# Sorting edges in a graph network: row one-hots turned from key columns by TensorE, lane one-hots scaled by ScalarE, and one block for ranks, placement and scatters

## The chip, the core and the metric

The kernel runs on one core of a Trainium2 chip. The metric is the device time of one execution in microseconds (us). A core has five engines with instruction streams of their own: TensorE (PE; its weight loads are listed as PEld), VectorE (DVE), ScalarE (ACT), GpSimd (POOL) and SyncE (SP). They meet only through semaphores. A DMA is issued from an engine's queue and runs beside the engines.

## The reference, cut to what matters

```
x:   (6250, 128) float32          src: (100000,) int32, random in 0..6249
dst: (100000,) int32 in 0..6249, sorted, dense at small numbers
edge_index = jnp.stack([src, dst])
h = jnp.maximum(_layernorm(x, axis=-1), 0.0)
x = x + _L0_gnn_ref(h, edge_index, ...)   # two GATv2 layers with self loops, softmax and sum over dst
h = jnp.maximum(_layernorm(x, axis=-1), 0.0)
x = x + _L1_gnn_ref(h, edge_index, ...)   # 8-head attention, sum over src (rows = edge_index[0])
```

The first part sums over the edges of each destination, the second over the edges of each source. The kernel therefore first brings the edges into two orders. Nothing of this order is in the reference: it is the kernel's way of doing the segment sums, and the change touches this sort alone.

## The kernel before, in words

The 100,000 edges lie as 800 columns of 125 edges, with the edge inside a column on the partition. A node number is split in a block (the number divided by 128, 49 of them) and a lane (the remainder). `sort_by_dst` finds for every edge a slot in a table in DRAM, `rec_by_dst`, in which the edges of a block of destinations lie together. It works in blocks of the program (`with nc.Block()`); every engine waits at the end of each for all others.

1. Keys are loaded and turned (about 8 to 28 us of the span), then counted (to 205 us), then tables are made (to 213 us).
2. **The ranks**, L448 to L578. A *half* is four columns, and there are 200 halves. For each half, VectorE makes one-hots in two layouts: `key_columns` (L538) compares a row of keys that SyncE has broadcast to all partitions with the partition's number (lane on the partition, edge along the row, 128x512), and `one_hots` (L529, through the helper's L301) compares keys on the partition with a row of numbers (edge on the partition), for the lanes (125x512) and for the blocks (125x196). TensorE matches the key columns with themselves (`match_keys`), adds the half to a running table (`update`), looks slots up in the table (`look_up`) and adds what lies earlier in the same column (`count_earlier`). ScalarE rounds the table (`round_table`, L476) and turns the match into 0 and 1 (`mark_earlier`, L466). VectorE takes the table's remainder (`split_table`, L551), multiplies the looked-up rows with the block one-hot (`read_table`, L558) and sums them to slots (`slots`, L564). `ranked` is raised by one with each half.
3. **Scans**, `SortBySrc.on_vector` and its sisters, in the same block after the ranks: for each of the 49 blocks of sources ScalarE makes a one-hot of 125x800, VectorE scans (L696) and multiplies (L699) it, and TensorE adds it up.
4. **The placement**, `SortBySrc.permute`, in a block of its own: for each of the 800 columns VectorE makes two lane one-hots, each multiplied with one piece of the edge's record (L763, 125x128), and a tile one-hot (L765, 125x832), and TensorE multiplies them in four matmuls (L805). This is the order by source, kept in SBUF.
5. **The scatters**, on POOL's queue. 49 indirect DMAs (L574) write the self loops' records into `rec_by_dst`. Then `Records.write` (L593) issues 800 indirect DMAs (L600), one for each column, 125 records of 8 bytes each. A scatter waits for its half's `ranked`, and for the scatter 16 before it to have landed. 320 of them are issued in the block of ranks and scans, the other 480 in the block of the placement.

What sets the order on each engine is the code's order. `pipeline` runs a list of stages for each half or column with a lead: a stage with lead 1 works on the next half. The first and last turns are unrolled, the rest is a loop of 8 halves (4 columns in the placement). No planner moves anything.

Each engine stalls only at its own waits, so the end of a block is the latest end of POOL's scatters, VectorE's chain, and what hangs on it. After the sort come the two graph layers, which read `rec_by_dst`.

## Time and profile before

| | us |
|---|---|
| median of 3 runs (7204.37, 7215.49, 7318.86) | 7215.49 |
| the profiled execution's own time | 7202.38 |
| its span, from the first to the last instruction | 7200.5 |
| the sort's last two blocks (ranks and scans; placement) | 213 to 926 and 926 to 1686 |

A row of a timeline gives start, duration, engine, line, operation, out<-in with shapes, the count of instructions merged in the row, and in brackets the idle time before it with what ended it. "issue" is idle time for which the profile shows no releaser. "remote" is a releaser that the profile does not see on the core's own engines at that moment. An instruction's duration can overlap the next one's start on the same engine, so a step of a loop is read from start to start. A window row gives, for a stretch of the span, each engine's busy time and in brackets its number of instructions, then the granted TensorE clock as a share of 2.4 GHz, the DMA engines' busy share and GB/s.

### The profile page before, as it was taken

The page shows a single profiled execution, that of the slowest core. Times are in us where ns is not written, and L with a number is a line of the kernel's source. Part 1 is how long each engine was busy: PE and PEld are TensorE (multiplying, and loading weights), DVE is VectorE, ACT ScalarE, POOL GpSimd, SP SyncE. Part 2 cuts the span into 40 slices and gives each one's busy share as a digit, 9 for nine tenths or more (in the row PEclk, how much of TensorE's full clock was granted, in tenths as well). Part 3 has the DMA queues.
Part 4 walks back from the last instruction along what each step waited for, and adds up shares of the span by engine and source line. Part 5 has one row for each costly group of instructions (what it writes and reads, how often), then busy time and mean ns, then how long its engine had stood idle before and what let it go on. Part 6 is the DMA issues. An engine that isn't in the chain of part 4 may idle for free. (4 is left out here: it accounts for less than half of the span.)

```text
span 7200.5 us, 128816 instructions
## 1 busy us (share of the span) xinstructions
PE 5138.8 (71%) x22244; PEld 2877.3 (40%) x22245; DVE 5824.7 (81%) x13976; ACT 3716.2 (52%) x17417; POOL 3967.3 (55%) x3546
## 2 busy tenths in 40 slices
PE   3386589972588898988877889889885555445452
PEld 2254233321244444444443444444443344444442
DVE  9596899972599999999848999999996455555556
ACT  5142500001399999999738999999993200000000
POOL 0688868882266666656305665666650255555552
PEclk9975899985799999999989999999997776776765
DMA  0234000001355555555424555555560233333333
GB/s 12 31 66 47 6 1 1 1 3 41 113 138 139 138 140 140 140 138 139 77 71 130 139 139 139 139 138 140 139 126 21 79 95 97 96 97 97 98 96 59
DMA packets 397679, 657.24 MB, mean 91 GB/s; under 512 B 141671, under 2 KB 259365, under 8 KB 396947
## 3 DMA queue, kind: packets, MB, share of 16 engines
q0 software_dynamic: 185888, 481.62, 27.2%
q1 hardware_dynamic: 211442, 172.59, 9.9%
q14 instruction: 326, 2.66, 0.2%
q8 instruction: 23, 0.38, 0.0%
HBM read 617.73 MB, written 33.88 MB: 90 GB/s over the span
## 5 line engine op out<-in xcount | busy, mean ns | idle before, releaser
L1209 POOL DMA_INDIRECT feat_area<-xl_table,feat_area x1856 | 1984.9, 1069 | 1721.1 <-PE bank L1283 680.1
L1360 ACT ACTIVATE feat_area<-feat_area 128x130 f32<-128x130 f32 x5568 | 1642.7, 297 | 181.2 <-issue 119.3
L1270 PE MATMUL bank<-node_area,feat_area 128*128 x3712 | 1470.2, 519 | 353.8 <-DVE feat_area L1405 158.5
L1344 ACT ACTIVATE feat_area<-feat_area 128x128 f32<-128x128 f32 x4640 | 1443.0, 387 | 64.6 <-issue 64.4
L1283 PE MATMUL bank<-feat_area 128*128 128x390 f32 x3712 | 1408.5, 502 | 68.1 <-ACT feat_area L1344 21.8
L1772 POOL DMA_INDIRECT feat_area<-kv_table,feat_area x832 | 809.8, 973 | 899.7 <-DVE feat_area L1869 352.5
L600 POOL DMA_INDIRECT rec_by_dst<-feat_area,gather_col x800 | 1123.0, 1404 | 281.3 <-issue 240.1
L1360 ACT ACTIVATION_READ_ACCUMULATOR feat_area<-feat_area 128x1 f32 x5568 | 1040.0, 187 | 26.9 <-issue 26.4
L1270 PEld LDWEIGHTS bank<-node_area,feat_area 128*128 128x128 f32 x3712 | 637.4, 191 | 997.9 <-issue 732.5
L1405 DVE TENSOR_TENSOR feat_area<-bank,feat_area 128x780 f32<-128x780 f32 x928 | 886.0, 955 | 65.1 <-remote 41.0
L1283 PEld LDWEIGHTS bank<-feat_area 128*128 128x128 f32 x3712 | 666.6, 190 | 645.8 <-issue 246.3
L1810 PE MATMUL bank<-feat_area 128*128 128x136 f32 x1664 | 388.9, 403 | 714.0 <-DVE feat_area L1869 672.4
L1413 DVE SCALAR_TENSOR_TENSOR feat_area<-feat_area 128x780 f32<-128x780 f32 x928 | 886.4, 955 | 0.0
L1822 ACT ACTIVATE feat_area<-feat_area 128x32 f32<-128x32 f32 x208 | 47.7, 229 | 1370.1 <-DVE feat_area L1857 754.0
L1886 DVE TENSOR_TENSOR node_area<-node_area,bank 128x136 f32 x832 | 242.5, 291 | 506.2 <-issue 160.6
L805 PE MATMUL bank<-feat_area 125*128 125x416 f16 x3200 | 636.5, 343 | 8.3 <-DVE feat_area L765 8.3
L1810 PEld LDWEIGHTS bank<-feat_area 128*128 128x128 f32 x1664 | 332.0, 288 | 764.2 <-DVE feat_area L1869 355.8
L1452 DVE SCALAR_TENSOR_TENSOR node_area<-node_area,stays,bank 128x390 f32 x812 | 493.8, 608 | 21.1 <-PE bank L1283 20.3
L1010 ACT ACTIVATE node_area<-node_area 128x6272 f32<-128x6272 f32 x2 | 10.9, 5429 | 815.7 <-DVE node_area L976 815.7
L763 DVE TENSOR_SCALAR feat_area<-feat_area 125x128 f16<-125x128 f16 x1600 | 419.4, 346 | 0.3
L805 PEld LDWEIGHTS bank<-feat_area 125*128 125x128 f16 x3200 | 248.4, 98 | 396.6 <-DVE feat_area L765 185.7
L957 DVE TENSOR_TENSOR feat_area<-iota_f,lo_col 128x256 f32<-128x256 f32 x928 | 379.8, 409 | 0.0
(313 smaller groups left out, 6762.8 us busy)
## 6 DMA issues: line engine op xcount, KB each, us to landing
feat_area<-lo_slot SPq DMA_DIRECT2D x464, 128.0 KB
feat_area<-xl_table,feat_area POOLq DMA_INDIRECT x1856
feat_area<-lo_slot_src SPq DMA_DIRECT2D x208, 128.0 KB
node_area<-lo_edge SPq DMA_DIRECT2D x100, 256.0 KB
xl_table<-feat_area SPq DMA_DIRECT2D x98, 195.0 KB, 2.2
feat_area<-kv_table,feat_area POOLq DMA_INDIRECT x832
rec_by_dst<-feat_area,gather_col POOLq DMA_INDIRECT x800
feat_area<-gates SPq DMA_DIRECT2D x348, 32.0 KB
```

What stands on the lines that cost most here:

```text
L600: pool.indirect_dma_start(k.rec_d, bass.IndirectOffsetOnAxis(ap=self.pos[:, c:c + 1], axis=0), self.pay[:, c, :], None).then_inc(self.writ ...
L805: last = nc.tensor.matmul(out[n][m], self.to_lane[s][:, n * P:(n + 1) * P], self.to_tile[s][:, m * half:(m + 1) * half], start=False, stop ...
L1209: pool.indirect_dma_start(ring[:, at:at + HE], None, k.xl, bass.IndirectOffsetOnAxis(ap=index[s // CG][:, n:n + 1], axis=0)).then_inc(gath ...
L1270: last = nc.tensor.matmul(pair[s % 2][:, u, 0:HE], pick[s // 2 % 2][:, c:c + P], k.node[:, ds(columns[0], HE)], start=True, stop=True)
L1283: last = nc.tensor.matmul(sums_in[s % 2], place[s % 2][:, u * P:(u + 1) * P], ring[:, at:at + HE], start=u == 0, stop=u == GS - 1)
L1344: last = nc.scalar.activation(row[:, 0:D], row[:, 0:D], ACT.Copy, scale=row[:, D:D + 1])
L1360: last = nc.scalar.activation(at, at, ACT.Copy, accum_out=score[s // CG][:, to:to + 1])
L1405: nc.vector.tensor_tensor(z[s % V].rearrange("p (u e) -> p u e", u=GS), pair[s % 2][:, :, 0:HE], ring[:, s * W:(s + 1) * W].rearrange("p ( ...
L1413: nc.vector.scalar_tensor_tensor(out=zu, in0=zu, scalar=0.0, in1=att_w.unsqueeze(1).to_broadcast([P, GS, HE]), op0=ALU.max, op1=ALU.mult). ...
L1452: last = nc.vector.scalar_tensor_tensor(out=k.node[:, ds(to, HE)], in0=spare, scalar=k.stays[:, ds(g, 1)], in1=sums_in[s % 2], op0=ALU.mul ...
L1772: pool.indirect_dma_start(kv[s][:, u * KV:(u + 1) * KV], None, k.kv, bass.IndirectOffsetOnAxis(ap=index[s][:, u:u + 1], axis=0)).then_inc( ...
L1810: nc.tensor.matmul(k.bank[2 + u][:, 0:VW], place[s % 2][:, u * P:(u + 1) * P], wv[s % 2][:, u * VW:(u + 1) * VW], start=True, stop=True).t ...
```

## The change

Three edits are made together.

1. **Ranks.** VectorE no longer makes the 125x512 lane one-hot. TensorE turns it from the key columns (`flip_keys`, four matmuls with the identity into one of two banks) and ScalarE copies it from the bank to SBUF (`keep_rows`). The key columns are made two halves ahead, in four buffers in place of two.
2. **Placement.** VectorE makes one unscaled lane one-hot per column (`at_lane`); ScalarE multiplies it with each of the two pieces (`scale`), and TensorE waits for that as well.
3. **One block.** Placement runs behind ranks and scans in the same block on every engine, and POOL's 800 scatters follow each other without a block's end among them.

The diff, without regard to indentation, cut to its core:

```diff
-RANK_COLS = 320
...
-    oh_loT = [cut(HALF * P // 2, F16) for _ in range(2)]
+    oh_loT = [cut(HALF * P // 2, F16) for _ in range(4)]
...
+    flip = [k.bank[n][:, 0:HALF * P] for n in range(2)]
+    move_on_vector, move_on_scalar, move_on_tensor, move_on_sync = beside.permute()
...
+            def keep_rows(j, s):
+                h = R * j + s
+                act.wait_ge(flipped, h + 1)
+                if later(h, 2):
+                    act.wait_ge(updated, h - 1)
+                nc.scalar.copy(oh_lo[s % 2].rearrange("p u m -> p (u m)"), flip[s % 2]).then_inc(lo_set, 1)
...
-            pipeline(act, halves, [(0, round_table), (0, mark_earlier)], R)
+            pipeline(act, halves, [(0, round_table), (1, keep_rows), (1, mark_earlier)], R)
             beside.on_scalar(act)
+            move_on_scalar(act)
...
+            def flip_keys(j, s):
+                h = R * j + s
+                pe.wait_ge(ohT_ready, h + 1)
+                if later(h, 2):
+                    pe.wait_ge(lo_set, h - 1)
+                for u in range(HALF):
+                    last = nc.tensor.matmul(flip[s % 2][:, u * P:(u + 1) * P], oh_loT[s % 4][:, u * P:(u + 1) * P], eye,
+                                            start=True, stop=True)
+                last.then_inc(flipped, 1)
...
-            pipeline(pe, halves, [(0, update), (0, look_up), (0, count_earlier), (1, match_keys)], R)
+            pipeline(pe, halves, [(1, flip_keys), (1, match_keys), (0, update), (0, look_up), (0, count_earlier)], R)
             beside.on_tensor(pe)
+            move_on_tensor(pe)
...
-                c = snapped(dve, HALF * h)
-                one_hot_rows(oh_lo[s % 2], lo, c, P)
-                one_hot_rows(hi3[s % 2], hi, c, NB).then_inc(oh_set, 1)
+                one_hot_rows(hi3[s % 2], hi, snapped(dve, HALF * h), NB).then_inc(hi_set, 1)
...
-            pipeline(dve, halves, [(0, split_table), (-1, read_table), (1, key_columns), (-1, slots), (1, one_hots)], R)
+            pipeline(dve, halves, [(0, split_table), (-1, read_table), (2, key_columns), (-1, slots), (1, high_rows)], R)
             beside.on_vector(dve)
+            move_on_vector(dve)
...
-            records.write(pool, 0, RANK_COLS, ranked)
+            records.write(pool, ranked)
...
-                    for n in range(2):
-                        nc.vector.tensor_scalar(self.to_lane[s][:, n * P:(n + 1) * P], self.iota[:, 0:P],
-                                                self.lane_f[:, ds(c, 1)], self.piece[n][:, ds(c, 1)], ALU.is_equal, ALU.mult)
+                if later(c, 4):
+                    dve.wait_ge(scaled, c - 3)
+                nc.vector.tensor_scalar(self.at_lane[s], self.iota[:, 0:P], self.lane_f[:, ds(c, 1)], None, ALU.is_equal
+                                        ).then_inc(lane_set, 1)
...
+                pe.wait_ge(scaled, c + 1)
...
+            def scale(j, s, c):
+                act.wait_ge(lane_set, c + 1)
+                if later(c, 4):
+                    act.wait_ge(moved, c - 3)
+                for n in range(2):
+                    last = nc.scalar.activation(self.to_lane[s][:, n * P:(n + 1) * P], self.at_lane[s], ACT.Copy,
+                                                scale=self.piece[n][:, ds(c, 1)])
+                last.then_inc(scaled, 1)
...
-        by_src.permute(records)
```

How it moves instructions, first on VectorE, in one half of the ranks. Names that begin with `r_` are semaphores of that block (`r_looked` is raised by `count_earlier`, `r_bc0` by the landing of a broadcast key row). Line numbers of the changed kernel are its own. Before:

```order
L551 TENSOR_TENSOR node_area<-bank,node_area 128x196 [waits r_looked,r_coarse]
L558 TENSOR_TENSOR node_area<-bank,node_area 125x196 [waits r_ranked,r_looked]
L544 TENSOR_SCALAR node_area<-node_area,part_f 128x512 [waits r_bc0,r_looked]
L564 TENSOR_REDUCE gather_col<-node_area 125x4 [waits r_multiplied]
L301 TENSOR_TENSOR node_area<-iota_b,node_area 125x512 [waits r_multiplied,r_looked]
L301 TENSOR_TENSOR node_area<-iota_b,node_area 125x196
```

And now:

```order
L571 TENSOR_TENSOR node_area<-bank,node_area 128x196 [waits r_looked,r_coarse]
L578 TENSOR_TENSOR node_area<-bank,node_area 125x196 [waits r_ranked,r_looked]
L564 TENSOR_SCALAR node_area<-node_area,part_f 128x512 [waits r_bc0,r_looked]
L584 TENSOR_REDUCE gather_col<-node_area 125x4 [waits r_multiplied]
L300 TENSOR_TENSOR node_area<-iota_b,node_area 125x196 [waits r_multiplied,r_looked]
```

The 125x512 comparison is gone, the other five operations of a half stand in the same order, and the key columns (L564 of the changed kernel) are for one half later.

On TensorE, one half of the ranks before, from the match for the next half on (L490 and L493 match, L502 updates, L510 and L513 look up, L520 counts):

```order
L490 MATMUL bank<-node_area 128x512 [waits r_earlier,r_onehotT]
L493 MATMUL bank<-node_area 128x128 x4
L502 MATMUL bank<-node_area 128x49 [waits r_fine,r_onehot]
L502 MATMUL bank<-node_area 128x49 x3
L510 MATMUL bank<-node_area 128x196 [waits r_multiplied]
L513 MATMUL bank<-node_area 128x49 x8
L520 MATMUL bank<-node_area 128x49 [waits r_earlier]
L520 MATMUL bank<-node_area 128x49 x3
```

And now, from the flip on (L502 flips, L510 and L513 match, L523 updates, L531 and L534 look up, L541 counts):

```order
L502 MATMUL bank<-node_area 128x128 [waits r_lo_rows,r_onehotT]
L502 MATMUL bank<-node_area 128x128 x3
L510 MATMUL bank<-node_area 128x512 [waits r_earlier]
L513 MATMUL bank<-node_area 128x128 x4
L523 MATMUL bank<-node_area 128x49 [waits r_fine,r_lo_rows,r_onehot]
L523 MATMUL bank<-node_area 128x49 x3
L531 MATMUL bank<-node_area 128x196 [waits r_multiplied]
L534 MATMUL bank<-node_area 128x49 x8
L541 MATMUL bank<-node_area 128x49 [waits r_earlier]
L541 MATMUL bank<-node_area 128x49 x3
```

Four matmuls are added ahead of the match, with a wait for ScalarE's copy of two halves ago, and the update waits for `r_lo_rows`, ScalarE's copy for this half, besides VectorE's two results.

On VectorE in the loop of the placement, one column before (ISA rows load a column's number):

```order
L763 ISA [waits p_moved]
L763 TENSOR_SCALAR feat_area<-feat_area 125x128
L763 ISA
L763 TENSOR_SCALAR feat_area<-feat_area 125x128
L765 ISA
L765 TENSOR_SCALAR feat_area<-feat_area 125x832
L761 REGISTER_ALU
```

And now, with the beginning of the next column:

```order
L779 ISA [waits p_scaled,p_moved]
L779 TENSOR_SCALAR feat_area<-feat_area 125x128
L781 ISA
L781 TENSOR_SCALAR feat_area<-feat_area 125x832
L776 REGISTER_ALU
L779 ISA [waits p_scaled,p_moved]
```

One of three comparisons is gone, and there is a wait for ScalarE (`p_scaled`) beside the one for TensorE.

## Rows read from the trace of the kernel before

**Rows 1.** The page's head and part 1, busy time and share of the span.

```profile
span 7200.5 us, 128816 instructions
...
PE 5138.8 (71%) x22244; PEld 2877.3 (40%) x22245; DVE 5824.7 (81%) x13976; ACT 3716.2 (52%) x17417; POOL 3967.3 (55%) x3546
```

**Rows 2.** Windows: stretch, length, PE, PEld, DVE, ACT, POOL, clock, DMA, GB/s.

```profile
277.00:301.60 24.60, 2.05 (x22) 1.36 (x22) 2.08 (x7) 1.13 (x3) 14.16 (x12) 1.00 0.08 1
...
301.60:577.00 275.40, 230.89 (x3017) 153.47 (x3016) 274.98 (x825) 119.28 (x275) 233.32 (x139) 0.75 0.42 67
...
577.00:773.00 196.00, 116.16 (x1273) 77.91 (x1274) 119.84 (x345) 52.05 (x117) 157.93 (x126) 0.54 0.32 35
...
779.50:896.00 116.50, 65.56 (x156) 27.20 (x156) 113.74 (x80) 75.05 (x78) 104.51 (x40) 0.97 0.05 1
...
935.00:1572.00 637.00, 635.58 (x3197) 248.07 (x3198) 636.64 (x2401) 0.00 (x0) 514.78 (x402) 1.00 0.08 1
...
1584.00:1677.00 93.00, 0.00 (x0) 0.00 (x0) 0.00 (x0) 0.00 (x0) 73.87 (x63) 0.50 0.10 3
```

**Rows 3.** Timeline of POOL: three scatters, after two waits and the last.

```profile
301.63 1.18 POOL L600 DMA_INDIRECT rec_by_dst<-feat_area,gather_col  x1 [6.90 <-DVE gather_col L564]
...
927.38 1.30 POOL L600 DMA_INDIRECT rec_by_dst<-feat_area,gather_col  x1 [31.25 <-ACTq L737]
...
1680.03 1.18 POOL L600 DMA_INDIRECT rec_by_dst<-feat_area,gather_col  x1 [0.30 <-issue]
```

**Rows 4.** Timeline of DVE: its first instruction after the placement's block.

```profile
1686.35 0.17 DVE L1036 MEMSET feat_area<- 128x128 f32 x1 [102.56 <-PEq L737]
```

**Rows 5.** Timeline of DVE: one half of the ranks' even stretch.

```profile
481.08 0.95 DVE L301 TENSOR_TENSOR node_area<-iota_b,node_area 125x512 bf16<-125x512 bf16 x2
481.95 0.35 DVE L551 TENSOR_TENSOR node_area<-bank,node_area 128x196 f16<-128x196 f32 x1
482.23 0.34 DVE L558 TENSOR_TENSOR node_area<-bank,node_area 125x196 f32<-125x196 f32 x1
482.50 0.41 DVE L544 TENSOR_SCALAR node_area<-node_area,part_f 128x512 f16<-128x512 f16 x1
482.83 0.34 DVE L564 TENSOR_REDUCE gather_col<-node_area 125x196 f32 x1
```

**Rows 6.** Timeline of POOL: a scatter of the even, one of the uneven stretch.

```profile
481.11 1.70 POOL L600 DMA_INDIRECT rec_by_dst<-feat_area,gather_col  x1 [0.30 <-issue]
...
599.74 1.18 POOL L600 DMA_INDIRECT rec_by_dst<-feat_area,gather_col  x1 [0.30 <-issue]
```

**Rows 7.** Who waited for whom in the ranks' uneven stretch, 577 to 773.

```profile
ACT node_area L466 <- remote: 93.8, 31, 5.7
```

**Rows 8.** Timeline of PE: the four 128-wide matmuls of two matches.

```profile
501.63 0.39 PE L493 MATMUL bank<-node_area 128*128 128x128 f16 x4
...
597.12 0.63 PE L493 MATMUL bank<-node_area 128*128 128x128 f16 x4
```

**Rows 9.** Timeline of DVE: one block of the scans and the next's begin.

```profile
887.37 1.88 DVE L696 TENSOR_TENSOR_SCAN feat_area<-feat_area 125x800 f32<-125x800 f32 x1
889.29 0.99 DVE L699 TENSOR_TENSOR feat_area<-feat_area 125x800 f32<-125x800 f32 x1
890.31 1.88 DVE L696 TENSOR_TENSOR_SCAN feat_area<-feat_area 125x800 f32<-125x800 f32 x1
```

**Rows 10.** Timeline of DVE: one column of the placement.

```profile
1563.92 0.53 DVE L763 TENSOR_SCALAR feat_area<-feat_area 125x128 f16<-125x128 f16 x2
1564.37 0.42 DVE L765 TENSOR_SCALAR feat_area<-feat_area 125x832 f16<-125x832 f16 x1
```

**Rows 11.** Window of L805 alone, early in the placement, PE catching up.

```profile
942.00:950.00 8.00, 8.00 (x45) 1.00 0.10 2
```

**Rows 12.** Timeline of ACT in a graph layer: six scaled copies.

```profile
3001.31 1.85 ACT L1344 ACTIVATE feat_area<-feat_area 128x128 f32<-128x128 f32 x6
```

**Rows 13.** Groups of instructions by line, ACT, 301 to 577.

```profile
L466 ACT ACTIVATE node_area<-bank 128x512 bf16<-128x512 f32 x138 | 82.4, 597 | 137.3 <-PE bank L493 103.8 <-issue 18.9 <-PE bank L520 14.6
```

## Prediction: what the change does to the time

> **What bounds the kernel now.** I read the page's head, then windows by stage, then the timelines of POOL and VectorE where stages meet. The page gives a span of 7200.5 us, and POOL only 55% busy over the whole of it [rows 1]. The share misleads: within the sort POOL is the engine that ends last. The windows show it [rows 2]. VectorE is full in the ranks' even stretch (275.0 of 275.4 us), in the scans and in the placement (636.6 of 637), and has nothing from 1584 on, while POOL goes on with scatters. Its last one starts at 1680.03 [rows 3], and VectorE's next instruction, in the next block, at 1686.35 after 102.6 us of idle time [rows 4]. So VectorE's chain is some 100 us early, and a microsecond taken from it is worth nothing by itself. What counts is how fast POOL gets through 800 scatters, and that depends on what VectorE does beside them:
>
> - nothing or little beside: 1.18 us and 0.30 to the next one, **1.48**, in the second row of [rows 6] and after 1584 [rows 2];
> - the ranks' even stretch: 1.70 + 0.30, the first row of [rows 6], 139 scatters in 275.4 us, **1.98**;
> - the scans: 40 in 116.5, **2.91** [rows 2];
> - the placement: 402 in 637, **1.585** [rows 2].
>
> And 31.25 us pass with no scatter at all: the first 320 are through, and the other 480 wait for the block's end [rows 3].
>
> Why 2.00 in the ranks: VectorE's half lasts 2.00 us [rows 5]. The scatter starts 0.03 us after the 125x512 comparison of L301. The pair under L301 takes 481.08 to 481.95; the 196-wide operations behind it are 0.27 to 0.28 apart, so the wide one takes 0.59. The scatter lasts 0.52 longer than alone: it stands until the wide comparison is over. In the scans the same: a scan and its product take 2.94 from start to start [rows 9], and POOL gets one scatter through in each.
>
> The Trainium skill has a rule for this ("SBUF — State Buffer", section "Who interferes with whom"): a VectorE instruction with two SBUF inputs contends with a GpSimd instruction that reads SBUF. L301, L696 and L699 read two SBUF operands, and the rows above agree.
>
> **The change, part by part.** I follow the changed program from 301.6, where the scatters begin to flow (12 are done by then [rows 2]) and take its start as it was.
>
> *Ranks, VectorE.* The wide comparison goes: 2.00 − 0.59 = 1.41 us a half. *ScalarE* had 119.28 us in 275 instructions, 0.87 a half; a copy of 128x512 from a bank is added, at 0.597 as L466 of the same shape [rows 13]: 1.46. *TensorE* had 230.89 us in 138 halves, 1.67 with the clock between its levels (0.75 of 2.4 GHz [rows 2]), and gets four matmuls, 0.39 us at the higher and 0.63 at the lower level [rows 8]: 2.06 to 2.30 as an upper bound, since ends are modelled and overlap. So a half lasts 1.46 to 2.30 us. I take 1.7, nearer to the lower end, since matmuls that overlap cost less than their sum. 197 halves end at 301.6 + 335 = 636.5. The added handing over (key columns, flip, copy, update) is made a half ahead on every engine, so it isn't in a half's chain as long as signals come at once.
>
> *Ranks, POOL.* Without the wide comparison a scatter takes between 1.48 (no contention) and 2.00 (it meets something else, once a half). I take 1.6: what is left are operations of 0.26 to 0.34 us, one of them with two SBUF inputs, and where VectorE does only such short ones, in the placement, a scatter takes 1.585. That gives 335 / 1.6 = 209 scatters.
>
> *The block's end.* The scans are unchanged: 6.5 us ahead of them, then 49 x 2.94 = 145 us. POOL gets 4 + 49 scatters, where before it had 39 and then a pause of 31 us. Behind them, until the first column of the placement, 12 us as before, now with 8 scatters. The pause itself is thus worth only 10 scatters, 16 us: it lay where scatters are slowest.
>
> *Placement.* VectorE: 0.79 us a column now (0.44 for two narrow comparisons, 0.35 for the wide one [rows 10]), 0.57 with one narrow one. ScalarE: two scaled copies of 128 at 1.85 / 6 = 0.31 [rows 12], 0.62. TensorE: 45 matmuls in 8 us while it catches up at the full clock [rows 11], 0.71 for four. TensorE is the limit: 800 x 0.71 = 568 us instead of 637. VectorE gets gaps, so I take 1.57 a scatter, between 1.48 and 1.585: 362 scatters.
>
> *The sum.* By the placement's end, 301.6 + 335 + 6.5 + 145 + 12 + 568 = 1368, there are 12 + 209 + 4 + 49 + 8 + 362 = 644 scatters. 156 are left at 1.483: 231 us. End at 1599 instead of 1681: **82 us less**. VectorE's last 12 us and the tables that SyncE stores hide under these 231 us; so does all of the placement's gain. The self loops' scatters, DMA landing and the code behind the sort don't change.
>
> The sum starts from the profiled execution, 7202.4 us: 7202.4 − 82 = **7120 us**. That execution stands 13 us under the median of the runs shown (7215.5); I don't add that, since the lowest run (7204.4) stands by it and the median of three is held up by one run at 7319.
>
> **The rivals.**
>
> *A. The scatters stay at 2.00 in the ranks.* What holds them could be another operation of the same half: the key columns' comparison (L544, 512 wide) takes 0.41, as long as the placement's of 832 [rows 5, 10], so something holds it up, and the scatter ends just then. Then 335 / 2.00 = 167 scatters in the ranks, and with 1.585 in the placement 598 by its end; 202 left take 300 us, end at 1668: 13 us less, 7189. Against it: the 0.52 us fit the wide comparison's length and place. The same page of the Trainium skill speaks for it (section "Who interferes with whom"): it infers that descriptor generation needs only the shared write interface, which a tensor_tensor doesn't take but a fast tensor_scalar such as L544 does. By that rule taking L301 away frees nothing, which is this case. The scans, where no tensor_scalar runs and scatters are slowest, speak against it.
>
> *B. Late signals, and the engines' chain becomes the bound: slower.* From 577 to 773 the ranks run unevenly, 58 halves (345 VectorE instructions, six each) in 196 us, 3.38 each, with VectorE and TensorE idle for 40% [rows 2]. ScalarE stands 93.8 us there for signals that the profile can't place [rows 7], at the lower clock (0.54 [rows 2]). I don't know what makes them late. The change adds two handings over between TensorE and ScalarE to every half. If each costs the 3.38 − 2.00 = 1.4 us that lateness costs now, and all halves run so, a half lasts 3.38 + 1.4 = 4.8: the chain of engines ends at 301.6 + 197 x 4.8 + 163.5 + 568 + 12 = 1991, and the time is 7202 + 1991 − 1681 = 7512. It begins to decide where this chain passes POOL, at 1045 + 197T = 1599, T = 2.8 us a half on average (2.39 now, of all 197), and costs 2% from T = 4.0. For it: the cause is unknown, and more signals cross. Against: only 58 of 197 halves run so now, the handings over are a half ahead, and TensorE will be busier, not idler.
>
> *C. The start stalls longer.* The first three halves take from 213 to 301.6, some 83 us more than 6 (VectorE busy for 2.1 of the last 24.6 [rows 2]); POOL waits only 6.9 us for them [rows 3], as the self loops' scatters cover the rest. The unrolled start now has one more pair of signals in it. If it costs half as much again, all comes 42 us later, 7162; if as much again, 83 us later, 7203, and the gain is gone.
>
> *D. Less contention than I take.* 1.48 in ranks and placement: 226 + 383 scatters, 118 left, end at 1543: 138 us less, 7064. Only the floor of all these terms reaches a gain of over 2%.
>
> *E. ScalarE bounds the placement.* If waits come on top of 0.62, say 0.9 us a column: the chain ends at 1532, still under POOL; more scatters are done by then. It costs nothing below 0.97 a column.
>
> **How the numbers follow.** The forecast (POOL is the bound, scatters eased, 7075 to 7180) gets 0.66, A 0.14, B 0.06, C 0.06, D beyond 7075 0.05, anything else 0.03. E changes only what is inside the forecast. The range takes in A and C and stops short of D's floor: 7075 to 7205. A measurement of this kernel can tell about 2% from no change, 144 us of 7215. Faster by over 2% would need a time under 7071, D nearly whole: 0.04. Slower by over 2%, over 7360: B: 0.05. Within: 0.91.
>
> **What the changed profile would show.** Right: 800 scatters without a pause of 31 us; in the ranks an average under 1.7 us from one scatter to the next; VectorE's five operations of a half with gaps; L805 at 0.70 to 0.72 us a column with VectorE no longer full; POOL still last, its last scatter near 1599, 200 us or more behind the placement. Wrong: scatters 2.00 apart in the ranks (A); halves of over 2.8 us on average, POOL waiting for `ranked`, and VectorE's chain ending with POOL's or later (B); the first scatter of a rank after 320 (C); a placement of over 0.97 us a column.

## The result, and the profile after

The changed kernel is **slower**: 7517.56 us, median of 4 runs (7512.47 to 7525.81), against 7226.85 for the kernel before, ratio 1.0425 (95% interval 1.039 to 1.046). Timed again twice, beside new runs of the kernel before, it was 1.0359 (1.0279 to 1.0439) and 1.0405 (1.0359 to 1.0451). I had forecast 7120 us in a range of 7075 to 7205.

The page's head and part 1 of the changed kernel, as [rows 1]:

```profile
span 7510.6 us, 135784 instructions
...
PE 5240.9 (70%) x23044; PEld 3042.2 (41%) x23045; DVE 5577.5 (74%) x12976; ACT 4351.2 (58%) x19217; POOL 3877.1 (52%) x3546
```

VectorE did lose 247 us of work and the span grew by 310: the time is in waits. The windows by stage, with the columns of [rows 2]; the first stretch is the ranks' even stretch of before:

```profile
301.60:577.00 275.40, 174.85 (x1846) 122.71 (x1846) 109.24 (x355) 100.52 (x214) 219.96 (x183) 0.55 0.31 36
577.00:1082.00 505.00, 310.20 (x3184) 215.83 (x3184) 185.69 (x614) 174.56 (x370) 402.95 (x336) 0.52 0.22 31
1087.00:1235.00 148.00, 81.49 (x198) 33.91 (x199) 142.52 (x102) 90.43 (x94) 132.16 (x53) 0.97 0.05 1
1260.00:1540.00 280.00, 175.86 (x765) 69.18 (x763) 123.56 (x382) 128.26 (x380) 222.64 (x189) 0.92 0.09 2
1580.00:1960.00 380.00, 380.00 (x2143) 208.35 (x2142) 320.38 (x1071) 350.45 (x1072) 0.00 (x0) 1.00 0.00 0
```

Read the counts. The ranks now end at 1082, not 773. In them 519 scatters in 780 us are 1.50 apart: nothing holds POOL any more, and VectorE is busy for 38%. In the placement, 191 columns (two operations of VectorE each) in 280 us are **1.47 us a column**, with TensorE busy for 63%; from 1580 on, in the same code, 535.5 columns in 380 us are **0.71**, with TensorE full. What ended in between is POOL:

```profile
1553.56 1.17 POOL L620 DMA_INDIRECT rec_by_dst<-feat_area,gather_col  x1 [0.30 <-issue]
```

Then VectorE's first instruction in the next block, as [rows 4]:

```profile
1984.14 0.17 DVE L1065 MEMSET feat_area<- 128x128 f32 x1 [3.92 <-PEq L446]
```

The roles have changed. POOL is through 126 us sooner than before (1680 [rows 3]) and nobody waits for it; the chain TensorE, ScalarE, VectorE ends 298 us later (1984 against 1686 [rows 4]). The balance: ranks +309, placement 725 us instead of 637, +88, and some 100 us back, since nothing runs on behind the placement. That makes 298 of the span's 310; the other 12 lie behind the sort.

Who waited for whom from 301.6 to 1082 (us in total, times, the longest):

```profile
ACT node_area L479 <- remote: 270.2, 102, 3.8
PEld bank L523 <- issue: 219.8, 144, 3.3
DVE node_area L578 <- PE bank L541: 164.0, 100, 2.8
...
DVE node_area L571 <- issue: 139.7, 93, 3.0
DVE node_area L571 <- ACT node_area L472: 115.5, 68, 3.0
```

All engines wait for each other, so none of them is the bound by its work, and much of the waiting is for what the profile can't name ("remote", "issue"). One such wait on the timeline, VectorE, TensorE and POOL:

```profile
693.74 0.53 PE L541 MATMUL bank<-node_area 125*128 125x49 bf16 x4
...
697.42 0.36 DVE L571 TENSOR_TENSOR node_area<-bank,node_area 128x196 f16<-128x196 f32 x1 [1.35 <-issue]
...
697.95 1.18 POOL L620 DMA_INDIRECT rec_by_dst<-feat_area,gather_col  x1 [0.30 <-issue]
...
699.29 0.36 DVE L578 TENSOR_TENSOR node_area<-bank,node_area 125x196 f32<-125x196 f32 x1 [1.50 <-PE bank L541]
```

L578 reads the look-up table of the half before that of L571, so the matmuls that it needs are those of 693.74 (VectorE's order is split_table of one half, then read_table of the half before). They were over by 694.3. VectorE is free at 697.8 and starts at 699.3. So 1.5 us are lost on something that was ready 5 us earlier. The starts also have a pattern, clearest for two operations: of the 32 times from 600 to 800 that L578 came after more than 0.7 us of idle time, 14 were 0.6 us behind a scatter's start and 18 were 1.3 to 1.5 behind it; of 24 such starts of L486 on ScalarE, 14 were at 0.5 to 0.6 and 10 at 1.3 to 1.4. The starts of L571 after such a wait lie elsewhere, most of them (31 of 39) 0.2 to 0.5 us behind a scatter's start. A scatter comes every 1.48 us.

**Theory S**: scatters that run back to back make the other engines' signals (or their issue) late. **Theory F**: the added handings over of the flip are slow themselves. **Theory C**: TensorE at its lower clock (0.52 to 0.55 here) is the bound.

Kernels are compared only with runs of the kernel before made beside them (one such set is a "call" in the expectations), since that kernel took 7187 to 7365 us (medians) in six sets and 6835 in one, the set of e6, e7 and e8, where signals were on time.

### The profile page after: what moved, and what is told of

It is laid out like the page before. It is cut to its first block and busy times, and to the rows that moved or that the text cites. A ratio compares the mean times of both kernels' runs of the same rounds, so it can differ in the third digit from the quotient of the medians.

```text
span 7510.6 us, 135784 instructions
## 1 busy us (share of the span) xinstructions
PE 5240.9 (70%) x23044; PEld 3042.2 (41%) x23045; DVE 5577.5 (74%) x12976; ACT 4351.2 (58%) x19217; POOL 3877.1 (52%) x3546
## 5 line engine op out<-in xcount | busy, mean ns | idle before, releaser
L620 POOL DMA_INDIRECT rec_by_dst<-feat_area,gather_col x800 | 1026.6, 1283 | 251.3 <-issue 239.1
L821 PE MATMUL bank<-feat_area 125*128 125x416 f16 x3200 | 614.3, 348 | 119.9 <-ACT feat_area L841 60.7
L841 ACT ACTIVATE feat_area<-feat_area 125x128 f16<-125x128 f16 x1600 | 527.6, 393 | 213.3 <-PE bank L821 112.6
L821 PEld LDWEIGHTS bank<-feat_area 125*128 125x128 f16 x3200 | 306.8, 99 | 427.4 <-DVE feat_area L781 172.2
L479 ACT CAST node_area<-bank 128x512 bf16<-128x512 f32 x200 | 117.9, 590 | 512.2 <-remote 309.1
L779 DVE TENSOR_SCALAR feat_area<-feat_area 125x128 f16<-125x128 f16 x800 | 228.2, 285 | 235.5 <-PE bank L821 163.6
```

Source lines behind the costliest of these rows:

```text
L620: pool.indirect_dma_start(k.rec_d, bass.IndirectOffsetOnAxis(ap=self.pos[:, c:c + 1], axis=0), self.pay[:, c, :], None).then_inc(self.writ ...
L821: last = nc.tensor.matmul(out[n][m], self.to_lane[s][:, n * P:(n + 1) * P], self.to_tile[s][:, m * half:(m + 1) * half], start=False, stop ...
L841: last = nc.scalar.activation(self.to_lane[s][:, n * P:(n + 1) * P], self.at_lane[s], ACT.Copy, scale=self.piece[n][:, ds(c, 1)])
```

## Experiments

### Scatters left out

e1 is the changed kernel without this statement and its waits; e2 the same of the kernel before.

```diff
-            pool.indirect_dma_start(k.rec_d, bass.IndirectOffsetOnAxis(ap=self.pos[:, c:c + 1], axis=0),
-                                    self.pay[:, c, :], None).then_inc(self.written[n], 16)
```

> The changed kernel without its 800 scatters of records and their waits: the sorted records are not written, everything else runs. Theory S (scatters that POOL starts back to back, one per 1.48 us, make the signals between TensorE, ScalarE and VectorE late): without them a half of the ranks lasts 1.5 to 1.8 us, the ranks end near 640 (1082 with them), the placement takes 0.71 us a column all the way (568 us), and the sort ends 600 us sooner, near 1370. Theory F (the two added handings over between TensorE and ScalarE are themselves slow): the halves stay near 4.1 us and the ranks end near 1080. Theory C (TensorE at its lower clock is the bound of the ranks): halves over 3 us as long as the granted clock shows 0.5.

> The kernel before without its 800 scatters of records and their waits: the records are not written, everything else runs. Theory S: no uneven stretch; all halves last 2.0 us or less, the ranks end at 695 or before (773 with scatters), the placement takes 0.79 us a column as before since VectorE sets it. If the uneven stretch has a cause of its own (a rival to S: the clock, or code that is loaded): 58 halves at 3.38 us remain and the ranks end near 770.

e1 took 6977.68 us and e2 7169.19 (one run each, the kernel before 7364.91 beside them). Only their sort is read: the layers behind it work on a table that was never written and take 5648 and 5693 us, where e3 and e4 beside them take 5555 and 5554. L571 (L551 before) runs once a half, so its first and last start give the ranks; L774 of e1 is the placement. e1, then e2:

```profile
L571 DVE TENSOR_TENSOR node_area<-bank,node_area x200: 351/362/363, 219.5 to 580.2; 128x196 f16<-128x196 f32 x100
L774 DVE TENSOR_SCALAR feat_area<-feat_area x800: 428/430/434, 741.8 to 1310.6; 125x832 f16<-125x832 f16 x160
```

```profile
L551 DVE TENSOR_TENSOR node_area<-bank,node_area x200: 342/343/362, 217.8 to 660.9; 128x196 f16<-128x196 f32 x100
```

Windows of e1, ranks and placement (columns as in [rows 2]):

```profile
320.00:570.00 250.00, 242.05 (x4337) 186.96 (x4336) 232.13 (x834) 216.61 (x502) 0.00 (x0) 1.00 0.29 87
760.00:1300.00 540.00, 540.00 (x3044) 296.08 (x3043) 455.24 (x1522) 498.20 (x1522) 0.00 (x0) 1.00 0.00 0
```

167 halves in 250 us: **1.50 us a half**, against 4.0 with them (194 in the 780 us above). Theory F falls: the flip's handings over cost nothing, and by itself the flip saves what was meant (e2's ranks, with VectorE full, go at 1.93). The uneven stretch of before is the scatters' work too: with them the ranks ended at 773, without at 663. The start stall also shrank in both: the even run begins near 285 instead of 301. What is left of it stands beside the self loops' 49 scatters, which are in all these kernels, 1.26 us apart until 275 in e1. Beside them e1 makes three halves in 65 us, and VectorE goes on only behind them:

```profile
279.84 0.36 DVE L578 TENSOR_TENSOR node_area<-bank,node_area 125x196 f32<-125x196 f32 x1 [33.62 <-remote]
```

That these scatters cause it wasn't tried by itself.

### The same code with and without scatters beside it

e3 holds the first scatter until all ranks are made, and leaves nothing out.

```diff
+        pool.wait_ge(ranked, COLS // 4)
         for c in range(COLS):
```

> The changed kernel with POOL's first scatter of a rank held until all 200 halves are ranked; nothing is left out. Theory S: halves of 1.5 to 1.8 us, ranks end near 640; then 800 scatters run beside scans and placement, 2.9 us each in the scans (some 50), and the placement takes 1.46 us a column all the way (800 columns, end near 1960), so the whole takes about 7500 us. Theory F: halves near 4.1 us, ranks end near 1080, the placement 1.46 us a column, the whole about 7950 us.

7532.21 us, one run. Ranks, then the placement while scatters run beside it:

```profile
L571 DVE TENSOR_TENSOR node_area<-bank,node_area x200: 351/361/363, 219.1 to 580.2; 128x196 f16<-128x196 f32 x100
...
760.00:1840.00 1080.00, 631.60 (x2526) 228.09 (x2527) 384.28 (x1264) 435.98 (x1265) 861.33 (x718) 0.88 0.09 2
```

As S has it: the loss moved with the scatters. The ranks are as quick as without any, and the placement now pays: 632 columns in 1080 us, 1.71 each (more than the 1.46 I had expected), at a granted clock of 0.88. That speaks against C: TensorE is busy for 58% there, so the clock isn't what a column waits for. In the ranks of the changed kernel, too, TensorE is busy for 62% (485 of 780 us) at its lower clock.

### The parts of the change by themselves

p1 is the kernel before in one block, p2 the kernel before with the flipped ranks alone, p3 with ScalarE's scaling alone. p1's and p2's cores:

```diff
-            records.write(pool, 0, RANK_COLS, ranked)
+            records.write(pool, ranked)
...
+            move_on_vector(dve)
```

```diff
-                one_hot_rows(oh_lo[s % 2], lo, c, P)
...
+                nc.scalar.copy(oh_lo[s % 2].rearrange("p u m -> p (u m)"), flip[s % 2]).then_inc(lo_set, 1)
```

> The kernel before with its two blocks made one, nothing else: POOL's scatters go on through the end of the scans. Theory S (scatters make the other engines' signals late): POOL is still last; its pause of 31 us goes, the last scatter comes near 1650 instead of 1680, ranks end near 773 and the placement keeps 0.79 us a column since only VectorE's own rate sets it: 20 to 31 us faster, ratio 0.996. Rival (one block is itself what disturbs the ranks): ranks end later than 800 and the time is above the one before.

> The kernel before with the ranks of the changed one alone (TensorE turns the one-hots, no wide comparison), two blocks and the placement as before. Theory S: the first 320 scatters run back to back at 1.48 us until about 755, halves 4.1 us each until then (some 115), the other 85 halves 1.5 us each, ranks end 870 to 890; placement at 0.79 us a column from about 1045, 480 scatters at 1.58 end near 1810: 130 us slower than before, ratio 1.018. If only the placement and the one block cost the time: ranks end near 640 and the time is below the one before.

> The kernel before with the placement of the changed one alone (ScalarE scales the lane one-hots), two blocks and the ranks as before. Theory S: ranks end near 773; in the placement 480 scatters come 1.48 us apart until about 1650 and a column takes 1.46 to 1.68 us beside them, the remaining 345 or so 0.71 us each: the placement ends near 1895, 215 us after the last scatter of before, ratio 1.03. If a column takes 0.71 us beside the scatters too: POOL is last, near 1650, and it is 30 us faster.

Ratios to the kernel before: **p1 0.9904** (0.9872 to 0.9937), **p2 1.0086** (1.0058 to 1.0115), **p3 1.0193** (1.0147 to 1.024). The first DVE instruction behind the sort comes 16 us sooner in p1, 101 later in p2, 183 later in p3 than in the profiled run of before; together 267 of the 298 that the whole change costs. For the rest there is a likely reason: in p2 POOL had to stop after its 320 scatters. (By medians p1 was 66 us quicker than the kernel before beside it, more than a pause of 31 us can give; the uneven stretch of the kernel before differs from run to run, see q2 below.) In p3 a column takes 1.43 us beside scatters. p2 shows the theory within one kernel:

```profile
320.00:740.00 420.00, 269.24 (x2800) 188.05 (x2798) 165.63 (x542) 152.81 (x326) 335.60 (x278) 0.53 0.32 35
770.00:870.00 100.00, 96.74 (x1736) 74.64 (x1734) 93.06 (x335) 86.74 (x201) 0.00 (x0) 1.00 0.31 84
```

Beside scatters 108 halves in 420 us, 3.9 each; behind the last one, in the same loop, 67 in 100 us, 1.5 each, and the clock back at 1.00. That speaks against C as well: the low clock goes with the gaps that the late signals leave, and the full clock is back when the scatters are over.

### More work for VectorE

If VectorE's wide comparison is what kept POOL at 2.00 us and the ranks even, putting it back should help.

```diff
+                one_hot_rows(unused[s % 2], lo, c, P)
                 one_hot_rows(hi3[s % 2], hi, c, NB).then_inc(hi_set, 1)
```

> The changed kernel with the wide comparison of before (125 x 512, two inputs) put back on VectorE in each half, into a tile that nothing reads: work added, none taken away. Theory S: it holds each scatter by 0.5 us as before, scatters come 2.0 us apart, the signals are on time in most halves, 2.0 to 2.6 us each, ranks end between 700 and 820, and the kernel is faster than the changed one, 7150 to 7270 us. Theory F: halves stay at 4.1 us or grow by the 0.8 us of VectorE, ranks end at 1080 to 1240, 7510 to 7670 us.

In the ranks it didn't: they end at 1090 (1082 in the changed kernel). The whole took 7578.89 us, ratio 1.0267 (1.0228 to 1.0305); the changed kernel wasn't run beside it, so its 1.036 to 1.0425 can't be set against this. The windows say why, the whole and one stretch in it:

```profile
320.00:1080.00 760.00, 422.33 (x4758) 292.93 (x4758) 387.90 (x1099) 259.44 (x549) 612.86 (x484) 0.58 0.30 32
650.00:700.00 50.00, 37.99 (x646) 27.99 (x647) 49.08 (x148) 32.39 (x72) 42.31 (x26) 1.00 0.50 67
```

From 650 to 700 it runs as hoped: 25 halves, 2.0 us each, one scatter to a half. Elsewhere (158 halves and 458 scatters in the other 710 us) 4.5 us a half and 2.9 scatters in each, of which the comparison can hold one. So there are two ways in which this loop runs: one scatter a half, held in step, or back to back. My reading, which no run isolates: the wide comparison keeps the first only while it lasts; once halves are late POOL gets ahead, and they stay late. It would also explain why the ranks of before ended at 773 in one profile and at 837 in another (q2).

### Fewer records, fills, fewer in flight

Records (e5, 16 of 125), fills (e6 and r2) and one scatter in flight (e7 and r3):

```diff
-            pool.indirect_dma_start(k.rec_d, bass.IndirectOffsetOnAxis(ap=self.pos[:, c:c + 1], axis=0),
+            pool.indirect_dma_start(k.rec_d, bass.IndirectOffsetOnAxis(ap=self.pos[0:FEW, c:c + 1], axis=0),
```

```diff
+            k.nc.gpsimd.memset(k.node[:, NODE_W - BUSY:], 0.0).then_inc(k.filled_pool, 1)
```

```diff
-DEEP = 16
+DEEP = 1
```

> The changed kernel with each of its 800 scatters cut to 16 of its 125 records (the others are not written). Two forms of theory S. S1, POOL's own work on a scatter holds the signals up, whatever it moves: the scatters come a little closer (1.1 to 1.4 us), halves stay at 3 us or more, ranks end after 900, a column of the placement takes over 1.1 us. S2, the transfers that a scatter starts hold them up: with an eighth of the transfers halves are at 1.5 to 1.8 us, ranks end 590 to 640, columns 0.71 us.

7862.35 us, one run: worse than whole scatters. Ranks end at 1561, 6.5 us a half, and POOL now waits for ranks (four scatters to each half). S2 is out as it was put. S1 had the ranks right (3 us or more, end after 900), though not how bad they are; its column can't be read, since the last scatter (1574) comes before the placement (1723). The bytes went down, the packets didn't: 32 for each scatter (24320 for 761), as in the changed kernel (16169 for 505). What went up is how close the scatters follow: each is 0.84 us long, and they come in bursts. One of 12, with ScalarE and VectorE beside it, then the next one's first:

```profile
796.78 0.84 POOL L621 DMA_INDIRECT rec_by_dst<-feat_area,gather_col  x1 [0.30 <-issue]
797.92 0.84 POOL L621 DMA_INDIRECT rec_by_dst<-feat_area,gather_col  x1 [0.30 <-issue]
...
808.23 0.83 POOL L621 DMA_INDIRECT rec_by_dst<-feat_area,gather_col  x1 [0.30 <-issue]
...
808.34 0.59 ACT L480 CAST node_area<-bank 128x512 bf16<-128x512 f32 x1 [10.84 <-remote]
812.55 0.60 ACT L487 ACTIVATE node_area<-bank 128x512 bf16<-128x512 f32 x1 [3.63 <-remote]
...
813.40 0.36 DVE L572 TENSOR_TENSOR node_area<-bank,node_area 128x196 f16<-128x196 f32 x1 [10.93 <-ACT node_area L473]
...
815.38 0.84 POOL L621 DMA_INDIRECT rec_by_dst<-feat_area,gather_col  x1 [6.32 <-DVE gather_col L585]
```

In the burst scatters are 1.15 us apart and the loop all but stops: three halves take almost 20 us (VectorE's L572 at 793.65 and at 813.40). It stays stopped when POOL is through (809.1), although nothing is at work then, and the match that ScalarE's L487 waits for was over by 807.9:

```profile
810.00:812.50 2.50, 0.00 (x0) 0.00 (x0) 0.00 (x0) 0.00 (x0) 0.00 (x0) 0.50 0.00 0
```

So whatever holds the signals up runs on for some 3.5 us behind the last scatter. It isn't chance: behind all 53 bursts of ten scatters or more, VectorE's next L572 starts 3.4 to 5.4 us after the last scatter's end (median 4.0). One match of e5 on TensorE, in the same burst:

```profile
802.82 0.31 PE L514 MATMUL bank<-node_area 128*128 128x128 f16 x1
803.43 0.26 PE L514 MATMUL bank<-node_area 128*128 128x128 f16 x1 [0.29 <-issue]
805.52 0.27 PE L514 MATMUL bank<-node_area 128*128 128x128 f16 x1 [1.83 <-issue]
807.62 0.27 PE L514 MATMUL bank<-node_area 128*128 128x128 f16 x1 [1.83 <-issue]
```

These four follow each other with no wait in the program, and before the third and the fourth 1.83 us pass. No packet of an instruction queue falls in this stretch (796 to 813), so it isn't code that is being loaded. So "late signals" is too narrow a name: instructions that wait for nothing start late as well. The Trainium skill says that the PE and ACT never wait on anyone ("SBUF — State Buffer", section "Who interferes with whom", on ports); if that holds for ports, this stall isn't one of a port.

> The changed kernel with each of the 800 scatters replaced by a fill of 1200 float32 columns by POOL in on-chip memory, one waiting for the one before (the sorted records are not written): POOL is as busy, and starts no transfer. S1, an instruction of POOL's, whatever it is, holds the signals: halves at 3 us or more, ranks end after 850, a column of the placement over 1.1 us. S2, it takes a scatter (its descriptors or its transfers): halves 1.5 to 1.7 us as without scatters (1.48), ranks end at 580 to 630, columns 0.71 us.

> The changed kernel with each scatter replaced by a fill of 1200 float32 columns by POOL, again. Where the kernel before takes about 6835 us: as the first time, halves of 1.8 us, columns of 1.25 us beside fills (VectorE's own comparison took 1.22 us instead of 0.43 beside them) and 0.71 after. Where it takes 7200 us or more: S1 (any work of POOL's makes signals late): halves over 3 us, ranks end after 850. S2 (it takes a scatter): the same 1.8 us a half and the ranks end at 580 to 640.

e6 was run in the set in which signals were on time and tells nothing of S1 and S2; r2 (7162.48 us, the kernel before 7204.16) does. Ranks of r2, and a window in them:

```profile
L572 DVE TENSOR_TENSOR node_area<-bank,node_area x200: 346/351/364, 219.2 to 649.0; 128x196 f16<-128x196 f32 x100
...
320.00:640.00 320.00, 268.86 (x4469) 199.81 (x4467) 316.34 (x859) 223.50 (x516) 304.82 (x264) 0.99 0.23 70
```

POOL is busy for 95%, and a half takes 1.86 us, bound by VectorE at 99%: it takes a **scatter**, not a busy POOL. S1 falls in that ("an instruction of POOL's, whatever it is"), and S2 holds in it. With e5: it is scatters, and how close they follow matters, not how many bytes they move.

> The changed kernel with one scatter in flight instead of 16: POOL waits for each to land before it starts the next, so scatters come further apart, at an estimate 2.5 to 3.5 us. If signals are late only while POOL works on a scatter, each scatter costs the ranks the 0.92 us that it costs now (500 us for 546 scatters): with 3 us between them a half takes 1.48 / (1 - 0.92 / 3) = 2.1 us, ranks end near 720. If it is the transfer in flight that makes signals late, they are late all the time: halves at 4 us or more, ranks end at 1080 or later. POOL is last either way and the whole is slower, over 8000 us.

> The changed kernel with one scatter in flight, again. Where the kernel before takes 7200 us or more: if a scatter costs the ranks the 0.92 us it costs back to back, halves of 1.48 / (1 - 0.92 / 4.7) = 1.84 us, ranks end near 655, and a column of the placement takes 0.71 / (1 - 0.86 / 4.7) = 0.87 us; if signals are late as long as a transfer is in flight, they are late all the time: halves of 4 us or more, ranks end at 1080 or later, columns of 1.46 us throughout. Where the kernel before takes about 6835 us: as the first time, ranks end near 524, columns of 0.71 us.

e7 (9328.87 us) was in the set with signals on time, too. r3 (9744.6 us, POOL last by far, the kernel before 7187.05) wasn't. Its ranks, a window in them, one in the placement, and a scatter:

```profile
L571 DVE TENSOR_TENSOR node_area<-bank,node_area x200: 348/361/364, 219.8 to 602.8; 128x196 f16<-128x196 f32 x100
...
320.00:600.00 280.00, 258.34 (x4535) 196.96 (x4533) 248.06 (x874) 224.43 (x524) 56.44 (x47) 1.00 0.39 79
900.00:1300.00 400.00, 400.00 (x2255) 219.33 (x2254) 342.17 (x1128) 365.44 (x1128) 95.42 (x79) 1.00 0.03 0
...
409.19 1.18 POOL L620 DMA_INDIRECT rec_by_dst<-feat_area,gather_col  x1 [4.33 <-DMA rec_by_dst<-feat_area,gather_col]
```

With scatters 5.9 us apart in the ranks and 5.0 in the placement, nearly always one in flight, halves take 1.60 us and columns 0.71: **next to nothing**, where 0.92 us for each scatter was expected. Against the 1.50 of e1 it is 0.1 us a half, at most 0.4 us for each of the 47 scatters, and in the placement nothing. A scatter has no fixed price: what it costs grows as scatters follow each other more closely.

### One scatter a half

```diff
-            if c % 4 == 0:
-                pool.wait_ge(ranked, c // 4 + 1)
+            if c < COLS // 4 or c % 4 == 0:
+                pool.wait_ge(ranked, max(c // 4 + 1, min(c + 1, COLS // 4)))
```

> The changed kernel with POOL held to one scatter a half in the ranks (scatter n waits for half n + 1, up to 200), all work done. By a cost of 0.92 us for a scatter: halves of 1.48 + 0.92 = 2.4 us, ranks end near 295 + 197 x 2.4 = 768 with 200 scatters done; then 50 in the scans, the placement starts near 930, 550 scatters at 1.48 us run beside it until 1744 with 1.46 us a column, and the rest at 0.71: end near 1905, some 60 us before the changed kernel: 7455 us. If a scatter that starts just after a half has ended holds up the next half more (as it stood where scatters had to wait for their ranks, 6.7 us a half with four scatters): 1.48 + 1.3 = 2.8 us a half or more, ranks end at 850 or later, 7500 us or more.

> The changed kernel with one scatter a half in the ranks, again. With signals late: between 7455 us (each scatter costs the ranks 0.92 us) and the changed kernel's own time or more. With signals on time: ratio 0.984 again, some 25 us behind the changed kernel, since POOL is last and starts its scatters later.

q3: 7379.67 us, ratio 1.0187 (1.0107 to 1.0266), beside 1.0359 for the changed kernel (q1) in the same set: 129 us better. Its window in the ranks:

```profile
320.00:680.00 360.00, 289.98 (x4420) 218.41 (x4419) 252.50 (x853) 224.00 (x512) 202.44 (x171) 0.88 0.44 64
```

171 halves, 2.1 us each, with as many scatters. Its ranks end at 700, before those of the kernel before (773), and what is left of the loss is in the placement, where scatters are back to back again: 979 us instead of 637. By distance, then, a half takes 1.50 us without scatters, 1.60 with them 5.9 apart, 2.1 at 2.1, 4.0 at 1.50, and at 1.15 (e5) the loop all but stands. e8 is the same kernel where signals were on time: 6725.56 us, ratio **0.9839** (0.9822 to 0.9855), and in its placement 0.71 us a column beside scatters 1.48 apart:

```profile
L781 DVE TENSOR_SCALAR feat_area<-feat_area x800: 422/431/855, 709.0 to 1278.1; 125x832 f16<-125x832 f16 x160
```

So back-to-back scatters are not enough by themselves; it also takes something that this one set didn't have. The set differed behind the sort as well: there e8 took 5153 us and q3, the same kernel, 5517. So 365 of the 651 us between their spans have nothing to do with the sort, and by an estimate from e8's 5153 the sort of the kernel before ended near 1680 there (6835 less 5153), about where it ends in its profile (1686): what it gained lay behind its sort.

### The first kernels again

> The changed kernel again, unaltered. If signals are late in this call (the kernel before near 7230 us or more): as the first time, ranks end near 1080, 1.46 us a column beside scatters, ratio 1.04. If they are on time (the kernel before near 6835 us): halves 1.5 us, ranks end near 530, the placement takes 0.71 us a column and ends near 1270, POOL is last with 800 scatters 1.48 us apart, 2.9 in the scans, from 280 to near 1535: 25 us before the paced kernel, some 6700 us, ratio 0.98. The rival, that the change is slower by its own work: ratio above 1 in both conditions.

> The kernel before again, unaltered, for its trace beside that of the changed kernel. With signals late: the start stall to 301 us, an uneven stretch in the ranks, ranks end near 773. With signals on time: no start stall (ranks from 220 on at 1.9 us a half, end near 605), the placement 0.79 us a column, POOL last near 1600 or later.

> The kernel before with its two blocks made one, again. With signals late: ratio 0.99 as the first time. With signals on time: POOL is last and loses only its pause between the blocks, at most 31 us: ratio 0.995 to 1.0.

> The changed kernel once more, unaltered. If the kernel before takes 7200 us or more in this call: ratio 1.036 to 1.045, columns of 1.46 us beside scatters. If it takes about 6835 us: halves of 1.5 us, columns of 0.71 us beside scatters, POOL last, about 25 us quicker than the kernel with one scatter a half was: ratio 0.98. Rival: ratio above 1 there too.

Four more with signals late. q1 and r1 repeat the first result (7508.41 and 7499.49 us; ranks end at 1071 and 1035, placement 733 and 748 us). q2 (7261.1 us) is the kernel before with a longer uneven run, ranks to 837. **q4, the kernel before in one block, is again the quickest: 7188.84 us, ratio 0.9943** (0.9904 to 0.9981). It beats both kernels, by little: this and p1's 0.9904 are under 2%, but both intervals lie below 1. Its last scatter:

```profile
L603 POOL DMA_INDIRECT rec_by_dst<-feat_area,gather_col x800: 1172/1283/2655, 277.8 to 1664.4; - x160
```

16 us ahead of the 1680.0 in the profile of before, which is what the prediction gave the pause; against q2, the kernel before beside it, it is 79 us, since q2's ranks end at 837 and q4's near 763. By medians q4 gains 26 us.

## Why the prediction was wrong

- **Ranks, VectorE and the other engines: the step that failed.** I took 1.7 us a half from the engines' work and set the added handings over at nothing "as long as signals come at once". As the engines' work the 1.7 was too high, if anything: 1.50 without scatters (e1). But beside scatters 1.50 apart a half took 4.0, and ranks meant to end at 636 ended at 1082. The 1.7 came from busy times, and the rows showed halves like those of now: the 58 at 3.38 us in the uneven stretch [rows 2], where scatters are 1.18 long [rows 6] and 1.56 apart. I read the quick scatters as a gain for POOL and the late signals [rows 7] as somebody else's trouble. They were one thing: without scatters the uneven stretch is gone (e2), and with the scatters held back the changed loop runs at 1.50 (e3). In the even stretch POOL was held at 1.98, in the uneven one it wasn't, and without the wide comparison the uneven stretch is the rule. (Putting the comparison back doesn't undo it, e4; pacing the scatters does for the ranks, q3.)
- **Ranks, POOL.** 1.6 expected, 1.50 measured, though beside a VectorE that stood for most of the time. The better proof is in runs without L301 whose ranks go quickly: a scatter is 1.18 us long there in q3 and 1.37 in e8 (medians), against 1.70 before, and the key columns' comparison is in both. So L301 did hold the scatters; rival A (2.00 stays) is out. By the rule of the Trainium skill that stood beside it ("SBUF — State Buffer", section "Who interferes with whom") taking L301 away would have freed nothing; the traces disagree.
- **Placement.** 0.71 us a column is exact for TensorE as the limit, but only behind the last scatter; beside them it is 1.47. The placement of before had no such trouble (0.79 beside scatters at 1.585 [rows 2]): one signal each way and four tiles deep. With ScalarE between VectorE and TensorE there is one more on the way, which is the likely reason. By the parts alone this mattered most: p3 costs 183 us, p2 101. In the whole change the ranks take most of the scatters and most of the loss (309 us, the placement 88).
- **"POOL is the bound".** True before, false after. POOL itself did better than the sum: its last scatter came at 1554, 45 us before 1599.
- **Rival B**, given 0.06, had the outcome: 7512 forecast, 7518 measured, its chain's end 1991, measured 1984. The closeness is partly luck. It put 4.8 us on a half (4.0 came) and 0.71 on a column (1.47 came), and laid the cost on the flip's handings over. e1 and e3 show that these cost nothing without scatters; but they are what the scatters make dear.
- **One block**: 16 us expected; the last scatter comes 17 and 16 us sooner than in the profile of before (p1, q4), the medians are 66 and 26 us lower. (The 39 scatters that the sum sets against 4 + 49 are those of the scans alone; from 773 to the pause it is 320 − 277 = 43 [rows 2], and with those the 10 come out.) **C** (a longer start stall) and **E** (ScalarE as the bound) didn't come.

**What stays open.** That closely spaced scatters slow the other engines is shown (e1, e3, p2, q3); how they do it isn't. It is not a busy POOL (r2), not the bytes they move (e5), not one transfer in flight (r3), and in two stretches not the loading of code: none of the 365 packets from 690 to 700 in the changed kernel, and none in e5's burst, belongs to an instruction queue. That the stall outlasts e5's bursts by 3.5 us looks like something that has to be worked off, no more. Nor is it known why one set had none of it. The changed kernel itself wasn't run there; that e8, its paced form, gained 1.6% makes it likely that it would gain too, no more. Two or three scatters in flight, between r3 and the rest, weren't tried, and neither was leaving out the self loops' scatters.

## What to carry to other kernels

An operation that holds another engine back may be doing the kernel a service: before taking it out, ask what the freed engine will do at full rate, and look for a stretch of the trace in which it already runs so. Two rates of one loop in one profile are such a stretch; price the change by the bad one too. And count the signals on the way of one item, not only the engines' busy times: beside back-to-back scatters the placement with ScalarE in it went from 0.71 to 1.47 us a column, the one without it stayed at 0.79.

## What the runs showed of the hardware that I had not expected

- Scatters 1.48 us apart took a loop of four engines from 1.50 to 4.0 us a half, scatters 5.9 us apart left it at 1.6, fills on POOL at 1.86. At 1.15 us (e5) it all but stopped, and stayed so for 3.5 us behind the last scatter.
- Two of the operations (L578, L486) then start at preferred moments of the scatter's period, 0.6 and 1.3 to 1.5 us behind its start, one of them on what was ready 5 us before.
- On the same chip and kernel (the one before) the median was 7261 us in one set of runs and 6835 in the next. In the quicker one signals weren't late in the sort (e8), but by the estimate above this kernel's gain lay behind the sort.
- A fill by POOL holds VectorE's comparison of 832 columns: 1.22 us instead of 0.43, in r2 from 900 to 1200:

```profile
L778 DVE TENSOR_SCALAR feat_area<-feat_area x232: 1220/1222/1223, 899.2 to 1199.5; 125x832 f16<-125x832 f16 x116
```
